# A decoder of two layers: the negated maxima of the second attention as two more rows of its query operand

## What is computed

```python
qkv = x @ W_attn + b_attn
q, k, v = jnp.split(qkv, 3, axis=-1)
q, k, v = (split_heads(q), split_heads(k), split_heads(v))
scores = jnp.einsum('bhqd,bhkd->bhqk', q, k) / jnp.sqrt(jnp.asarray(D, x.dtype))
scores = jnp.where(causal, scores, -jnp.inf)
probs = jax.nn.softmax(scores, axis=-1)
out = jnp.einsum('bhqk,bhkd->bhqd', probs, v)
out = out.transpose(0, 2, 1, 3).reshape(B, S, E)
return out @ W_proj + b_proj
```

## Time and profile before

| | us |
|---|---|
| median of three runs | 343.73 |
| the profiled execution | 344.39 |
| its span, first to last instruction | 342.6 |
| TensorE matmuls busy in the span | 258.0 (75%) |
| DVE busy | 216.6 (63%) |
| ACT busy | 148.1 (43%) |
| POOL busy | 67.2 (20%) |
| mean granted TensorE clock | 0.881 |

### The profile page before, as it was taken

One profiled execution on the slowest core, in us unless ns is written; L12 is line 12 of the kernel. 1 busy time (PEld: TensorE's weight loads), 2 busy tenths in 40 slices (PEclk: granted clock), 3 DMA queues, 4 the chain that ended last, 5 costly groups with the idle time before them and its releaser, 6 DMA issues.

```text
span 342.6 us, 6843 instructions
## 1 busy us (share of the span) xinstructions
PE 258.0 (75%) x2658; PEld 196.1 (57%) x2658; DVE 216.6 (63%) x538; ACT 148.1 (43%) x274; POOL 67.2 (20%) x102
## 2 busy tenths in 40 slices
PE   0855875997979998979896699999978767751530
PEld 0834674896868887878775476666655433340120
DVE  3992787449935799575554565667657576355562
ACT  4861553236513773623532344444514552301651
POOL 8900000000000200126201756413201000011001
PEclk9986989899989999999996999999999996655555
DMA  7956405142333305244400080004000000000011
GB/s 256 364 132 199 93 19 122 63 125 61 78 109 100 86 2 125 99 120 118 65 2 1 2 149 2 2 2 99 3 3 0 3 2 0 0 0 1 0 31 31
DMA packets 27679, 22.86 MB, mean 67 GB/s; under 512 B 19136, under 2 KB 24256, under 8 KB 26944
## 3 DMA queue, kind: packets, MB, share of 16 engines
q1 hardware_dynamic: 27648, 22.43, 25.3%
HBM read 12.20 MB, written 6.03 MB: 53 GB/s over the span
## 4 chain that ended last, share of the span: by engine, by line
PE 46%; DVE 25%; ACT 12%; DMA 7%; issue 6%; POOL 3%; ACTq 0%; DVEq 0%; POOLq 0%
DVE arena L1076 7%; DMA arena<-arena 6%; PE PS L506 4%; ACT arena L882 4%; PE PS L682 3%; PE PS L578 3%; PE PS L605 3%; ACT xt L905 3%; PE PS L546 2%; PE PS L704 2%; PE PS L547 2%; POOL rstd L433 2%; PE PS L532 2%; PE PS L688 2%; PE PS L687 2%
## 5 line engine op out<-in xcount | busy, mean ns | idle before, releaser
L431 POOL TENSOR_SCALAR shift<-mv 128x3 f32<-128x3 f32 (+2 forms) x15 | 3.6, 240 | 256.6 <-DVE mv L1138 256.6
L1076 DVE TENSOR_TENSOR arena<-PS,arena 64x512 f16<-64x512 f32 x64 | 44.0, 688 | 7.4 <-ACT arena L882 5.9
L882 ACT ACTIVATE arena<-PS 64x512 f16<-64x512 f32 x64 | 37.8, 591 | 24.9 <-PE PS L534 24.2
L532 PE MATMUL PS<-xh,w0l 128*128 128x256 f32 x64 | 22.4, 350 | 16.7 <-DVE w0l L1066 9.7
L961 ACT ACTIVATE PT<-PS 128x512 f32<-128x512 f32 x32 | 19.1, 596 | 34.4 <-PE PS L688 34.2
L905 ACT ACTIVATE xt<-res,shift,rstd 128x128 f32<-128x128 f32 x42 | 17.7, 483 | 32.6 <-POOL shift L434 32.5
L1211 DVE TENSOR_REDUCE rowmax<-PS 128x4 f32<-128x512 f32 x32 | 21.9, 688 | 13.7 <-PE PS L690 13.1
L1081 DVE TENSOR_REDUCE rowmax<-PS 128x4 f32<-128x512 f32 x32 | 21.9, 685 | 10.9 <-PE PS L547 10.8
L546 PE MATMUL PS<-arena 128*128 128x128 f16 x128 | 20.3, 239 | 8.4 <-DMA arena<-arena 8.0
L895 ACT ACTIVATE PT<-PS 128x512 f32<-128x512 f32 x32 | 19.1, 597 | 17.2 <-PE PS L562 15.9
L532 PEld LDWEIGHTS PS<-xh,w0l 128*128 128x128 f32 x64 | 14.0, 219 | 18.9 <-ACT w0h L870 9.6
(11 more groups left out here) (206 smaller groups left out, 663.8 us busy)
## 6 DMA issues: line engine op xcount, KB each, us to landing
arena<-arena SPq DMA_DIRECT2D x8, 512.0 KB, 4.2
v_piece<-VN SPq DMA_DIRECT2D x8, 512.0 KB, 2.9
V<-v_piece SPq DMA_DIRECT2D x64, 64.0 KB, 2.4
arena<-k_piece SPq DMA_DIRECT2D x4, 192.0 KB, 4.5
arena<-q_piece SPq DMA_DIRECT2D x4, 192.0 KB, 6.3
q_piece<-VN SPq DMA_DIRECT2D x6, 96.0 KB, 1.7
xT<-x_T SPq DMA_DIRECT2D x1, 512.0 KB, 4.1
w<-wk SPq DMA_DIRECT2D x2, 256.0 KB, 4.5
```

The source lines that it names most:

```text
L532: mm(dst, w0l[:, w, g], xh[:, x], start=True, stop=False)
L882: m = fn(dst[:, a], src[a * 64:(a + 1) * 64], ACT.Copy)
L1076: m = tt(lower[:, a], src[a * 64:(a + 1) * 64], upper[:, a], ALU.subtract)
```

## The change

The maxima reach the key-major scores by the contraction itself. The first half of each group's memset, which is the key stack, now writes the bit pattern of two f16 ones, the second half, the query stack, zero. Rows 32 and 33 of the query stack are spare; when the negated maxima of batch b are in MR, SP copies the high part's 16 rows into row 32 and the low part's into row 33, heads along the row, for the tokens of b (two transfers of 4 KB each). The key-major matmul, K against Q, then adds them, and the four selector matmuls are gone. TensorE waits for these transfers (max_in) in place of mr1_done. Query-major pieces of the batch are over by then.

KEYS_AT is 6 where 5 was written: the key-major pieces and all that follows from them stand one tick later, in the late part too. On SP the order of transfers is now walked through the ticks, so that the maxima stand among the loads of the stacks.

```diff
-            for h in MIDS:
+            def mid(h, i):
                 cols = slice(B0[h] * P, (B0[h] + N[h]) * P)
...
+            def place_maxima(b):
+
+                g = GROUP[b]
+                t = slice((b - B0[g]) * P, (b - B0[g] + 1) * P)
+                sp.wait_ge(s("mr1_done"), b + 1)
+                for i in range(2):
+                    sp.dma_start(Qst[g][32 + i:33 + i, :, t], MR[32 * i:32 * i + H, b % 2, :]).then_inc(s("max_in"), 16)
+
+            for t in range(T1 + TICKS1):
+                for k in range(3):
+                    for kind, g, i in TICKS.get((t, k), ()):
+                        if kind == "mid":
+                            mid(g, i)
+                for b in range(NB):
+                    if t - T1 - u1(b) == 4:
+                        place_maxima(b)
...
-                pool.memset(x, 0.0).then_inc(s(f"stack_zero{g}"), 1)
+                half = x.shape[1] // 2
+                pool.memset(x[:, 0:half], PAIR_OF_ONES)
+                pool.memset(x[:, half:2 * half], 0.0).then_inc(s(f"stack_zero{g}"), 1)
...
                 if of_keys:
-                    pe.wait_ge(s("mr1_done"), b + 1)
+                    pe.wait_ge(s("max_in"), 32 * (b + 1))
...
                     if of_keys:
-                        mm(part_, K[:, n, t], Q[:, n, t], start=False, stop=False)
-                        m = mm(part_, En[:, n, :], MR[:, b % 2, :], start=False, stop=(h == 3))
+                        m = mm(part_, K[:, n, t], Q[:, n, t], start=False, stop=(h == 3))
...
-                        for at, read in ((10, "on1_done"), (11, "onT1_done"), (12, "res1_done")):
-                            outs = len([c for c in range(NB) if u1(c) + at < u])
+                        for at, read in ((5, "on1_done"), (6, "onT1_done"), (7, "res1_done")):
+                            outs = len([c for c in range(NB) if u1(c) + KEYS_AT + at < u])
```

## The result

The changed kernel takes 364.3 us (median of four executions, 361.53 to 364.9), the kernel before 343.0 beside it: a ratio of 1.059 (95% interval 1.054 to 1.063), slower by 20 us. The forecast was 352.8, at most 356.5. The sign was right, and so was what the prediction thought the main cause; the sum was too small by more than half.

The account below looks back on a forecast made before the run. TensorE was taken to set the pace in the second attention (199 to 283 us). Terms -5.4 + 1.0 + 6.4 + 5.6 + 1.5 = +9.1 us gave a forecast of 352.8 us, range 344.5 to 356.5.

Parts of the forecast that it names:

- removed matmuls: TensorE, second attention: 128 selector matmuls gone from 32 key-major pieces, -5.4 us, with 3.5 and 7.1 as bounds.
- tick shift itself: Key-major work and all that follows, late part included, one tick later: priced at nothing.
- turns that wait for DVE: TensorE, turns of the maxima of batches 2, 3, 6 and 7: four times 0.25, +1.0 us (0 to 2).
- transfers of six batches: SP, maxima of batches 1, 2, 3, 5, 6 and 7: hidden within about two ticks, no cost.
- waits of batches 0 and 4: TensorE waits for maxima queued on SP behind stack loads: +6.4 us for batch 0, +5.6 for batch 4.
- clock behind these waits: TensorE slowed to 1.2 GHz after its two long waits: +1.5 us (0 to 3.4).
- cover of the tail: End of the key-major work: if this cover is gone, one piece and its exponential, 0.44 + 0.6 us.
- L688's share of the chain of waits: Selector line on TensorE, 199 to 283 us: 6.4% of the chain over 84 us, 5.4 us.
- order on SP: Maxima of batches 0 and 4 stand behind stack loads, landing at 207.1 and 242.4 us.
- The first rival: Small transfers pass the large ones, landing 1.6 us after their second issue: +1.5, 345.2 us; chance 0.17.
- idle time that it took off batch 0's wait: TensorE's existing idle before 199.24 us, 0.5 us, subtracted from a wait of 6.9 us.
- list of what would show it wrong: Profile signs: all pairs landing in 2 us, or no TensorE wait on them (wrong by 10 us or more).

Follow-up runs that it names:

- later late part: Kernel before with only the late part one tick later (groups 3 and 4 start at +14 and +12): 345.9 us, ratio 1.009.
- whole shift with its turns: Changed kernel's order, key-major side one tick later in all engines, but with selectors, the old wait and no transfers of maxima: 349.6 us, ratio 1.015.
- within the shifted order: Changed kernel's order with the tick shift, without selectors, transfers or their wait (maxima not subtracted): 347.9 us, ratio 1.010, against 349.6 with selectors.
- filled waits: Changed kernel with 28 and 22 filler matmuls on TensorE ahead of its waits for the maxima of batches 0 and 4: 358.6 us, ratio 1.044.
- batches 0 and 4 on selectors: Changed kernel, but batches 0 and 4 keep selector matmuls and have no transfers; the other six batches keep theirs: 347.2 us, ratio 1.011.
- experiment on ACT's queue: Changed kernel with the maxima transfers of batches 0 and 4 issued from ACT's queue in place of SP's: 354.0 us, ratio 1.032.

## Why the prediction was wrong

By its own steps, in its order:

| step | predicted | measured |
|---|---|---|
| removed matmuls | -5.4 | -2.4 alone, -1.7 within the shifted order |
| tick shift itself | 0 | +3.1 for the later late part, its clock included; +5.1 for the whole shift with its turns |
| turns that wait for DVE | +1.0 | +1.0 in the trace's waits |
| transfers of six batches | 0 | nothing that can be told |
| waits of batches 0 and 4 | +12.0 | +11.6 (filled waits against batches 0 and 4 on selectors) |
| clock behind these waits | +1.5 | +4.9 |
| sum | +9.1 | +20.1 |

The last two terms and the 3.6 of the kernel without long waits make 20.1 by the way they are formed. What is tested are the parts of the 3.6: the shift's 5.1 less the 1.7 of the matmuls give 3.4.

**The failing step is the sentence "I price the shift itself at nothing".** It argued that the last tick more holds no work that was not there, and even with the cover of the tail gone it saw 1.0 us. The shift with its turns costs 5.1 us, not 1.0. A later tick moves the start of the late part, whose last chain, that of group 4, runs to the end of the program and was not shortened again; and the clock falls twice in the stretch ahead of it, where it did not before. How the 3.1 us divide between the two is open.

The turns came out at the 1.0 forecast by luck. Four times 0.25 was the sum; measured are 0.2 at batches 2 and 3, 0.7 at batch 7, 0.7 at batch 4, which the prediction did not have on its list, and 0.9 less at batches 5 and 6, where the list had batch 6 down for 0.25 more.

**The removed matmuls were mis-sized.** Taking L688's share of the chain of waits, 6.4%, for the gain assumes that what follows moves up by as much; it was 2.4 of 5.4, or between 1.1 and 3.8. These two steps and the turns together were put at -4.4, and the kernel that has them all and no long wait stands at +3.6: 8.0 of the 11 us by which the forecast fell short.

**The clock was under-sized.** The mechanism was right (0.50 behind both waits), but the prediction charged less than one slow stretch and the kernel after has 5.8 and 3.0 us of TensorE work at half speed; half of their 8.8 is 4.4, and 4.9 was measured. This is the other 3.4 us of the shortfall; the waits by themselves were 0.4 less than forecast. The prediction took TensorE behind the waits to be partly waiting for others; in the slow stretches after, it is busy without a gap (5.80 of 5.80 us and 2.95 of 3.00).

**Right:** the order on SP as the cause, the place and length of both waits (6.9 and 5.6 forecast, 7.06 and 5.94 in the trace), five of the six pairs that hide, and that the small transfers don't pass the large ones. The first rival is refuted by the changed kernel, and the experiment on ACT's queue refutes it for a queue of its own too. One reading was off by little: the idle time that it took off batch 0's wait is 0.32 us in the earlier trace rows, not 0.5. The prediction's list of what would show it wrong did not have the start of the late part on it.

## What to carry to other kernels

A small transfer took 1.7 us or 6 here according to what the DMA engines held when it was issued; put it on the queue ahead of the large loads whose data is needed later, and don't count on another queue while those loads run. When a step is moved by one tick, first ask which chain to the end of the program begins behind it, and at which clock the stretch ahead of it then runs, before you call the shift free. And the waits in which every engine stood still were paid again behind them, with 4.9 us of half-speed matmuls.

## What the runs showed of the hardware

- *Executions of one program differ together with the clock.* In 16 executions of the kernel before, each with its span and its mean granted clock, the spans go from 340.2 us at 0.890 to 343.3 at 0.876: 2.0 us for each 0.01, with a correlation of -0.96. Ten executions without selectors show 1.9 us for each 0.01. A difference of 1 us between two kernels is smaller than what this does between two executions of one, so a single pair of profiles can't show it.
- *An instruction load can sit in front of a small transfer.* Batch 3's second transfer landed after 3.1 us, and TensorE waited 1.3 us for it. The DMA queues from 229 to 235 us of the kernel after (packets, MB, share of 16 engines) show who was there too:

```profile
q8 instruction: 1, 0.02, 1.3%
```

  One packet of 16 KB, 1.27 us on one of the 16 engines (230.80 to 232.07); the other fifteen had their parts of both transfers landed by 232.1, and the last two parts landed at 233.3 and 233.5. TensorE waited for these, so one such packet on one engine is enough.
- *A 4 KB transfer occupies its queue for 0.5 to 0.6 us.* The sixteen issues of L374 took 0.50 to 0.60 us each, one of them 0.96, and so more than a load of 192 KB, of which two are issued in 0.84. The two transfers of a batch thus start 0.6 us apart, and TensorE waits for the second.
